# A fused attention, expert and FFN kernel: causal masks as matrix products, maxima of two heads in one pass, and three steps moved

## What is computed

```python
x = x + gated_experts(layernorm(x), token_ids, ctx)       # stage a: expert chosen by token id
x = x + block(layernorm(x), ...)                          # stage b: attention, then MoE (m)
x = x + wkv(layernorm(x), ctx, w, u)                      # stage c: a decaying scan over time
x = x + ffn(layernorm(x), w1, w2)                         # stage d: 8-bit activations, ternary weights

# block, shortened
attn = einsum('bqhd,bkhd->bhqk', q, k) / sqrt(16)          # 16 heads of 16
attn = where(causal, attn, -inf)
h = einsum('bhqk,bkhd->bqhd', softmax(attn), v)
x = residual + h @ Wo.T
logits = rmsnorm(x) @ Wr.T                                 # top 2 of 8 experts, 512 wide
```

## Time and profile before

| | |
|---|---|
| runs, us | 510.27, 509.72, 516.72 (median 510.27) |
| the profiled execution | 516.34 us, of which the span below is 514.6 |
| PE busy | 369.4 us, 72% of the span |
| DVE, ACT, POOL busy | 261.3, 152.8, 222.3 us |
| mean granted clock of PE | 0.793 of full speed |
| PE in the chain that ended last | 53%; DVE 18%, POOL 10% |

### The profile page before, as it was taken

How to read it: one execution, slowest core, us unless ns; L and a number is a source line. 1 busy time by engine, 2 the same in 40 slices (tenths; PEclk the granted TensorE clock), 3 DMA queues, 4 the chain that set the end, 5 groups by cost and what they waited for, 6 DMA issues and landing times.

```text
span 514.6 us, 6681 instructions
## 1 busy us (share of the span) xinstructions
PE 369.4 (72%) x2042; PEld 282.0 (55%) x2045; DVE 261.3 (51%) x780; ACT 152.8 (30%) x332; POOL 222.3 (43%) x338
## 2 busy tenths in 40 slices
PE   0776999648797877764353399999999535757765
PEld 0555787326565655443342288887788314646454
DVE  4578896654354672514720032333232157998652
ACT  2221243113342425410020134333243311233563
POOL 2482443402232444615277208676930188423530
PEclk9997899757757667755556599999999955786799
DMA  8900029967180004000033334326000132000011
GB/s 260 394 11 1 0 94 155 150 138 120 44 120 25 3 2 144 20 1 20 1 84 109 52 121 176 134 79 221 34 26 29 37 90 62 1 1 0 4 37 42
DMA packets 16693, 39.18 MB, mean 76 GB/s; under 512 B 3314, under 2 KB 10804, under 8 KB 14868
## 3 DMA queue, kind: packets, MB, share of 16 engines
q1 hardware_dynamic: 11476, 30.63, 22.3%
q0 software_dynamic: 1872, 5.11, 3.9%
q10 hardware_dynamic: 3312, 3.02, 1.7%
HBM read 29.38 MB, written 9.31 MB: 75 GB/s over the span
## 4 chain that ended last, share of the span: by engine, by line
PE 53%; DVE 18%; POOL 10%; issue 7%; DMA 5%; ACT 4%; another core or an unknown queue 2%; SPq 1%; ACTq 0%; DVEq 0%; POOLq 0%
PE bank L1366 8%; PE bank L1368 7%; PE bank L1367 7%; PE bank L1372 6%; DVE junk L1045 4%; PE bank L1428 3%; POOL yc L629 3%; PE bank L1489 3%; PE bank L1553 3%; PE bank L1462 2%; PE bank L1525 2%; PE bank L1739 2%; PE bank L1537 2%; PE bank L1758 1%
## 5 line engine op out<-in xcount | busy, mean ns | idle before, releaser
L1241 DVE TENSOR_TENSOR act_lo<-bank,act_hi 128x512 fp32r<-128x512 f32 x23 | 15.9, 692 | 84.9 <-ACT act_hi L815 74.4
L1045 DVE CUSTOM_DVE_ANT_0 junk<-bank,causal 128x128 bf16<-128x128 f32 (+1 forms) x128 | 38.0, 354 | 28.0 <-PE bank L1489 28.0
L593 POOL TENSOR_SCALAR_AFFINE_SELECT E_sb<-E_sb 128x128 f32<-128x128 f32 x64 | 21.3, 333 | 71.5 <-ACT E_sb L773 71.4
L1366 PE MATMUL bank<-we_hi,xg_hi 128*128 x92 | 39.7, 432 | 9.8 <-DVE xg_lo L1235 8.2
L584 POOL TENSOR_TENSOR we_lo<-we_lo,we_hi 128x3072 fp32r<-128x3072 f32 x6 | 40.8, 6798 | 0.5
L1367 PE MATMUL bank<-we_lo,xg_hi 128*128 x92 | 37.3, 405 | 0.0
L1368 PE MATMUL bank<-we_hi,xg_lo 128*128 x92 | 37.2, 404 | 0.0
L1366 PE MATMUL bank<-we_hi,act_hi 128*128 x92 | 28.9, 314 | 10.7 <-DVE act_lo L1241 10.7
L773 ACT ACTIVATE E_sb<-bank 128x384 f32<-128x384 f32 x64 | 27.9, 488 | 24.0 <-PE bank L1507 22.6
L583 POOL TENSOR_SCALAR we_hi<-we_lo 128x3072 fp32r<-128x3072 f32 x6 | 17.0, 2828 | 36.3 <-DMA we_lo<-in_wexp 36.2
L629 POOL DMA_INDIRECT yc<-y_dram,pos_i x16 | 15.9, 991 | 35.7 <-DMA y_dram<-y_sb 31.7
(11 more groups left out here) (246 smaller groups left out, 1002.7 us busy)
## 6 DMA issues: line engine op xcount, KB each, us to landing
we_lo<-in_wexp SPq DMA_DIRECT2D x8, 1536.0 KB, 7.1
qk_dram<-qk_parts SPq DMA_DIRECT2D x8, 512.0 KB, 4.3
q_pack<-qk_dram SPq DMA_DIRECT2D x24, 128.0 KB, 4.6
k_pack<-qk_dram SPq DMA_DIRECT2D x24, 128.0 KB, 7.8
y_dram<-y_sb ACTq DMA_DIRECT2D x23, 128.0 KB, 1.7
we_hi<-in_w_t SPq DMA_DIRECT2D x2, 1024.0 KB, 11.1
ctx_sb<-in_ctx_t SPq DMA_DIRECT2D x1, 1024.0 KB, 5.4
xn_dram<-x_n SPq DMA_DIRECT2D x8, 128.0 KB, 1.8
```

The source lines that it names most:

```text
L593: g.affine_select(out=diag[:, 0:P], in_=diag[:, 0:P], compare_op=ALU.is_ge, fill=0.0, base=0, pattern=[[1, P]], channel_multiplier=-1)
L1045: last = v.tensor_tensor_reduce(out=junk[:, m % 2, t * P:t * P + keys], in0=row_banks(b)[h % 2][:, t * P:t * P + keys], in1=causal[:, 2 * ...
L1366: t_.matmul(dst, l_hi, r_hi, start=start, stop=False)
```

## The change

1. The causal mask is a bf16 tile of 384 columns in two forms (causal, causal_t), set up by POOL. Before each pair of row scores and before each pair of column scores PE multiplies it by the identity into both banks; the scores are accumulated on top. POOL's selects on E_sb and the semaphore mask_done are gone.
2. One plain maximum over a three-dimensional view of two banks does both heads; the eight PSUM banks are now one tensor.
3. In the lead, even pairs use banks 0 and 1, odd pairs banks 2 and 3, and a pair waits for the maxima of the pair before the last one. After it all use 2 and 3.
4. The order in the lead changes on PE, DVE and ACT (b_low, b_norm, b_stats, b_turn, b_turned); max_rows writes bank 7.
5. The pieces x transposes and router logits of the epilogue stand a step later, max_rows too.
6. Expert 2 is loaded after batch 1's column scores and split by DVE; pieces stand at steps 18 to 21, 22 to 25 and 26 to 29.
7. FFN: h and g have scales of their own; h is prepared three tiles ahead, in three buffers; on ACT the next h copy stands before the g copy, on PE g transposes come first, then the next h transposes, w2 and w1 products.

```diff
         LEAD = 12
-        NM_AT = {(b + 1) * HP - LEAD: b for b in range(1, B)}
+        NM_AT = {(b + 1) * HP - LEAD + 1: b for b in range(1, B)}
-        SPLIT_AT = [2 * HP, 3 * HP]
-        EP_OT, EP_HT, EP_WO, EP_RMS, EP_XT, EP_LG = 1, 2, 3, 4, 5, 6
+        SPLIT_AT = [2 * HP + 2, 2 * HP + 6, 3 * HP + 2]
+        EP_OT, EP_HT, EP_WO, EP_RMS, EP_XT, EP_LG = 1, 2, 3, 4, 6, 7
-        def row_banks(b):
-            return bank[0:2] if b == 0 else bank[2:4]
+        def row_banks(r):
+            return psum[:, 0:2, :] if r < LEAD and r % 2 == 0 else psum[:, 2:4, :]
+        def row_bank_free(r):
+            return 2 * (r - 1) if r < LEAD else 2 * r
...
# SP
+            sp.wait_ge(st_done, 2 * H)
+            load_expert(RING - 1)
             store_max(3)
             for i in range(TB, 2 * TB):
                 store_x2(i)
-            sp.wait_ge(st_done, 3 * H)
-            load_expert(RING - 1)
# POOL, set-up, then the loop
+            for c in (0, 2):
+                g.affine_select(out=causal_t[:, c * P:(c + 1) * P], in_=causal_t[:, c * P:(c + 1) * P],
+                                compare_op=ALU.is_ge, fill=-BIG, base=0, pattern=[[1, P]], channel_multiplier=-1)
+            for c in (0, 2):
+                last = g.affine_select(out=causal[:, c * P:(c + 1) * P],
...
-                if m < NP:
-                    for n in (2 * m, 2 * m + 1):
-                        pool.wait_ge(exp_done, n + 1)
...
-            pool.wait_ge(st_done, B * H)
-            split_expert(RING - 1)
# ACT
             b_high(4)
-            b_turned(6)
             b_high(5)
-            b_turned(7)
             nm_copy(0)
+            b_turned(6)
+            b_turned(7)
+            d_h_copy(0)
+            for step in range(NT + 2):
                 if step < NT:
-                    d_h_copy(step)
                     d_gelu_of(step)
+                if step + 1 < NT:
+                    d_h_copy(step + 1)
+                if step >= 2:
+                    d_g_copy(step - 2)
# DVE
+            def row_pair(r):
+                dve.wait_ge(s_done, 2 * r + 2)
+                for t in range(TB):
+                    last = v.tensor_reduce(negmax[:, b % 2, t, h:h + 2],
+                                           row_banks(r)[:, :, t * P:t * P + (t + 1) * P], AX, ALU.max)
+                last.then_inc(max_done, 2)
             row_pair(0)
             b_low(4)
+            row_pair(1)
+            b_stats(7)
+            for r in range(2, 6):
+                row_pair(r)
+            b_low(5)
+            for r in range(6, 8):
+                row_pair(r)
             b_norm(6)
+            row_pair(8)
             b_norm(7)
+            for r in range(9, LEAD):
                 row_pair(r)
+            for i in range(NT + 2):
+                if i < NT:
+                    d_g_scales(i)
+                if i + H_AHEAD < NT:
+                    d_h_scales(i + H_AHEAD)
+                if i >= 2:
+                    d_last(i - 2)
# PE
+                for odd in range(2):
+                    t_.matmul(row_banks(r)[:, odd, 0:3 * P], ident_b[:, :], causal[:, :], start=True, stop=False)
...
+                for odd in range(2):
+                    t_.matmul(bank[4 + odd][:, 0:3 * P], ident_b[:, :], causal_t[:, :], start=True, stop=False)
...
+            for r in range(2, 9):
                 score_row_pair(r)
             max_rows(0)
+            score_row_pair(9)
+            b_turn(6)
+            score_row_pair(10)
+            b_turn(7)
+            score_row_pair(11)
+            d_h_turn(0)
+            d_up_products(0)
+            for step in range(NT + 3):
+                if 2 <= step < NT + 2:
+                    d_g_turn(step - 2)
+                if step + 1 < NT:
+                    d_h_turn(step + 1)
+                if step >= 3:
+                    d_down_products(step - 3)
+                if step + 1 < NT:
+                    d_up_products(step + 1)
```

More of the change, by code:

```diff
@@ L520, in _ @@
             g.memset(causal[:, :], 0.0)
+            g.memset(causal_t[:, :], 0.0)
             g.memset(picked[:, :, :], 0.0)
@@ L666, in _ @@
             c_times_v(3)
-            for i in range(2, 4):
+            for i in range(2, 5):
                 rsqrt(4, i).then_inc(rstd_in[4], 1)
-            for step in range(NT + G_LAG):
-                d_round(step)
-                if step < 2:
-                    rsqrt(4, step + 4).then_inc(rstd_in[4], 1)
-                if step == 1:
-                    for i in range(6, 8):
-                        rsqrt(4, i).then_inc(rstd_in[4], 1)
+            for i in range(H_AHEAD):
+                d_round_h(i)
+                rsqrt(4, i + 5).then_inc(rstd_in[4], 1)
+            for i in range(NT):
+                d_round_g(i)
+                if i + H_AHEAD < NT:
+                    d_round_h(i + H_AHEAD)
         @block.scalar
@@ L902, in d_g_copy @@
                 last.then_inc(d_gtc, 1)
-            for step in range(NT + G_LAG):
+            d_h_copy(0)
+            for step in range(NT + 2):
                 if step < NT:
-                    d_h_copy(step)
                     d_gelu_of(step)
-                if step >= G_LAG:
-                    d_g_copy(step - G_LAG)
+                if step + 1 < NT:
+                    d_h_copy(step + 1)
+                if step >= 2:
+                    d_g_copy(step - 2)
         @block.vector
@@ L1088, in _ @@
                         quantise(step)
-            def row_pair(r):
-                for n in (2 * r, 2 * r + 1):
-                    row_max(n)
             a_others(7)
@@ L1097, in _ @@
             b_low(4)
-            b_norm(6)
-            b_stats(7)
-            row_pair(1)
-            row_pair(2)
-            b_low(5)
-            row_pair(3)
+            row_pair(1)
[5 more added lines that the diff above has]
+                row_pair(r)
+            b_norm(6)
+            row_pair(8)
             b_norm(7)
-            for r in range(4, LEAD):
+            for r in range(9, LEAD):
                 row_pair(r)
@@ L1349, in _ @@
                 c_result(i)
-                if i < 6:
-                    d_scales(i - 4)
-            for step in range(2, NT + G_LAG):
-                d_scales(step)
-                if step >= 5:
-                    d_last(step - 5)
-            for i in range(5, NT):
-                d_last(i)
+                if i < 4 + H_AHEAD:
+                    d_h_scales(i - 4)
+            for i in range(NT + 2):
+                if i < NT:
+                    d_g_scales(i)
+                if i + H_AHEAD < NT:
+                    d_h_scales(i + H_AHEAD)
+                if i >= 2:
+                    d_last(i - 2)
         @block.tensor
@@ L1467, in max_rows @@
                 pe.wait_ge(max_done, H * (b + 1))
+                if b == 0:
+                    pe.wait_ge(b_lo, 6)
+                elif b == 1:
+                    pe.wait_ge(b_lo, 2 * B)
+                else:
+                    pe.wait_ge(ep_htc, b - 1)
                 for t in range(TB):
-                    last = t_.transpose(row_banks(b)[0][0:H, t * P:(t + 1) * P], negmax[:, b % 2, t, :], ident[:, :])
+                    last = t_.transpose(bank[EP_Z][0:H, t * P:(t + 1) * P], negmax[:, b % 2, t, :], ident[:, :])
                 last.then_inc(nm_tr, 1)
@@ L1730, in d_h_turn @@
                     pe.wait_ge(d_htc, i)
-                transpose_d(bank[6], q_h[:, i % 2, :]).then_inc(d_htr, 1)
+                transpose_d(bank[6], q_h[:, i % H_BUF, :]).then_inc(d_htr, 1)
             def d_up_products(i):
```

141 lines of the change are left out of this document (56 added, 85 removed).

## The result

The changed kernel takes **481.45 us** (median of 4 runs, 481.44 to 485.4) beside 512.02 us for the kernel before on the same chip (median of 4, 509.72 to 516.72): ratio 0.941, 95% interval 0.932 to 0.950. The forecast was 481, its range 467 to 508. On another chip the same kernel took 463.04 us beside 492.11 (0.942, 0.933 to 0.952): the ratio repeats, the microseconds don't. Where the chips differ is told at the end.

The account below looks back on a forecast made before the run. TensorE was taken to bound the attention loop, with waits on VectorE in the lead and on ScalarE in the FFN. Terms 0.5 - 6 - 14 - 5 - 5 = -29.5 us, hung on the 510.27 us median, gave 481 us, range 467 to 508.

Parts of the forecast that it names:

- Lead: Row scores before the first column scores: two bank pairs start column pair 0 near 110.5 us, -6 us (bounds -3, -8).
- the larger of VectorE 1.11 and TensorE 0.82: Time per row pair before the attention loop at 2.4 GHz, with VectorE and TensorE overlapping: 1.11 us instead of 2.09.
- The lead stopped at pair 8 by the packs: Sign of being wrong: row pair 8 waits for batch 1's packed keys, which were forecast in by about 105 us.
- Price of a mask pair: Two added TensorE matmuls of 384 columns per score pair: 0.32 us at 2.4 GHz (at most 0.39), 0.64 at 1.2 GHz.
- Loop: Attention loop of 32 steps: 76.6 us of work at clock 0.92 plus 10 idle, 93.3 against 107.1 us, -14 us.
- clock stays: Rival: TensorE's loop clock stays at 0.69, loop 123 us (+16), whole 514 us; chance 0.13.
- clock falls: Rival: identity mask products pull TensorE's loop clock to 0.60, loop 140 us (+32.6), whole 530 us; chance 0.09.
- Tail: After the loop: without GpSimd's expert split, x_n -2.4, gate subtraction -1.7, last values no longer waiting for masks -1; -5 us.
- FFN: From 470 us to the end: a tile takes 3.3 to 3.5 us instead of 4.23, -5 us (bounds -6 and 0).
- Third expert's split: Moved from GpSimd's tail to VectorE's loop steps 26 to 29, 6.2 us: zero if it fits, +4 if not.
- waits change places: Rival: VectorE's splits, v_proj's wait and the exp chain keep loop idle at 20 us; loop -4, whole 491 us; chance 0.11.
- the stall moves: Rival: the unexplained stall at the experts' start depends on timing, 15 us more may go, whole 466 us; chance 0.05.

Follow-up runs that it names:

- the run with one: The changed kernel with all row pairs of the lead on one bank pair instead of two: 491.83 us, ratio 0.962.
- The runs without row masks: Two runs of the changed kernel: masks on the transposed scores alone, 476.26 us (ratio 0.929); no mask products at all, 482.32 us (0.926).
- the second time: The changed kernel, unchanged, measured and profiled again on another chip: 463.04 us beside 492.11 for the kernel before, ratio 0.942.
- Fillers: The changed kernel with 148 identity products of 384 columns into an unused bank, ahead of TensorE's waits behind the loop: 473.33 us beside 492.49, ratio 0.959.
- the first four experiments: Masks added to the kernel before (517.02 us); the changed kernel without masks (482.32), with masks on transposed scores alone (476.26), with one bank pair in the lead (491.83).

## Why the prediction was right, and where not

**Sum.** Forecast -29.5, measured -30.6 between the medians of the result and -34.9 between the two profiled executions (516.34 and 481.46). Every large term has the right sign, and the parts miss by -3 to +3 us each: lead 3.1 too little, loop 2.2, FFN 2.9 and tail 0.9 more than forecast, and 3.0 in the scan stage that are not the change's. That the median came within half a microsecond of the 481 is luck on top of a sound mechanism.

- **Lead: -6 forecast, -2.9 measured** from the first row pair on, at the small bound of -3 (column pair 0 starts at 112.87 instead of 116.50, not near 110.5). The two bank pairs bring 6.1 (the run with one). What failed is the step "the larger of VectorE 1.11 and TensorE 0.82": it holds for pairs 2 to 7 only. "The lead stopped at pair 8 by the packs", one of the signs of being wrong, came true. Behind the wait for the packs (4.70 us, at 105.53; the landing "by about 105" was right) the rest is TensorE's, in a row, at 1.2 GHz, with masks at 0.75 a pair. The start of column pair 0 was worked out from the maxima's round trip through memory, and no wait for it shows: TensorE's own queue ended last. The runs without row masks have a lead 3.1 and 3.6 us shorter. Nor was it foreseen that pair 2 starts at 94.84, not 97.12: from there to column pair 0 the change wins 1.4 us only (19.4 to 18.0).
- **Start: +0.5 forecast, -0.6 measured** (first row pair at 90.50 and 89.92; 91.35 the second time): a cost of GpSimd's added set-up can't be told from the spread.
- **Price of a mask pair: 0.32 forecast, 0.42 measured** (94.84 to 95.26, where the scores start), over the upper bound of 0.39. Fillers standing together take 4.06 / 24 = 0.17 us each at 2.4 GHz, so 0.34 for two: the columns were priced right. The other 0.08 appears only where scores with other weights follow; what in the switch takes it no run here parts. The page "TensorE: Matmul & The Clock Gate" of the Trainium skill, Part 2, Back-to-back issue gap, gives N / 2.4 + 2.5 ns for an isolated product of N columns, by which the two would take 0.325 us, an estimate; the fillers agree within 5%, the masks between scores don't, and the measurement decides. In the loop the 52 mask pairs made 22 us, not 16.6 (52 x 0.42, and the work of 81 less 59 without them).
- **Loop: -14 forecast, -16.2 measured.** The formula was work / clock + idle. Forecast 76.6 / 0.92 + 10 = 93.3; measured 81 / 0.98 + 6.6 = 89.1. Masks dearer by 4 to 5 us, clock better by 0.06, idle less by 3.4. Which part matters most only the experiments show: take the masks away and the loop still falls from 105.3 to 95.2 us, at a clock of 0.72; add them to the old loop and it falls to 100.5. The shorter waits are the larger part (the maxima a step later are worth about 4 us; how the rest divides between GpSimd's masks and the cheaper maxima is not shown), and the clock's gift is that 21 us of masks cost the loop little: nothing by the profiles (89.1 against 95.2), at most some 4 us by whole runs (8 us less the 3.6 of the lead).
- **Clock.** Expected from the 2 us slices, and shown: 0.69 to 0.92 by the masks alone. The rivals "clock stays" and "clock falls" are both out. That identity weights pull the clock down was drawn from a stretch of transposes; the same page of the Trainium skill, Part 4: PE-mode transpose, speaks of transposes, and the 0.50 slice of the earlier trace rows agrees with it, but it doesn't reach to an identity as weights of an ordinary product: 24 of them in a row ran at 2.4 GHz.
- **Tail: -5 forecast, -5.9 measured.** x_n 3.37 to 0.88, gate 1.89 to 0.17, both confirmed by undoing the move of the split.
- **FFN: -5 forecast, -7.9 measured**, beyond the bound of -6. The tile was set at 3.3 to 3.5 us because VectorE was counted at 3.3 busy, TensorE at 3.0. In the steady tiles (457.80 to 463.46) VectorE is busy 2.5 to 2.7 us a tile and TensorE all the time, 2.83: dividing a stage's busy time, with the scan's last results in it, by eight overstated VectorE. The old order gives 4.24 again.
- **Third expert's split:** none of TensorE's waits in the loop is for VectorE's pieces; the zero end.
- **Rival "waits change places"**: the named waits came, 6.3 us together, not 20. **Rival "the stall moves"**: TensorE waits 8.51 us for act_lo there, 8.67 before; it didn't move with the kernel (below).

## To carry over

Before masks, copies or other fixed work go to TensorE, read its clock: in a loop where it is full at half clock, full-width products can cost little or nothing, while the same products in front of a chain that alternates with another engine cost their full price, and at 1.2 GHz nearly twice that (0.75 us a pair instead of 0.42). Filler products pay only ahead of the wait that they are to cover, no longer than it, and only where TensorE's next work is on the path. When several engines are near the bound, price each stage as work / clock + idle and check both terms by an experiment, since a right total can hide wrong ones.

## What the hardware did that was not expected

- **The same program is 20 us faster on some chips, in one stage.** Experts: 144.5 to 146.3 us in the profiles of before and after and of the first four experiments, 124.8 to 125.9 in those of the others, on two other chips (130.3 with fillers in it). Total of the kernel before: 511 to 512 and 492 us. On the slower chips ScalarE and VectorE stand still with nothing that the profile shows as the cause ("remote"). ScalarE in the changed kernel:

```profile
248.30 0.60 ACT L810 ACTIVATE sil<-psum 128x512 f32<-128x512 f32 x1 [5.98 <-remote]
253.95 0.60 ACT L814 ACTIVATE act_hi<-psum 128x512 fp32r<-128x512 f32 x1 [5.05 <-remote]
265.26 0.38 ACT L805 ACTIVATE xg_hi<-psum 128x256 fp32r<-128x256 f32 x1 [10.71 <-remote]
```

  The 21.7 us of these three waits are about the difference. They are in the kernel before alike, so the change has no part in them; their cause stays open.
- **A large GpSimd operation can hold a small one of VectorE until it ends:** 1.89 us instead of 0.17 for the gate's subtraction, 3.37 instead of 0.88 for two x_n, seen in two kernels, each to within 0.3 us of the end of GpSimd's pass, and gone where GpSimd does not split after the loop. Other operations of VectorE beside the same pass took their usual time; which ones are held no run here varies.
